# First layer of a four-layer image kernel: the projection streams the image over four column quadrants of TensorE, VectorE turns 32x32 blocks, and TensorE sums the squares

## The chip, the cores and the metric

One NeuronCore of a Trainium2 chip runs the whole program. The metric is the device time of one execution in microseconds (us); less is better. A NeuronCore has TensorE (PE in the rows; its weight loads are PEld), VectorE (DVE), ScalarE (ACT), GpSimd (POOL) and SyncE (SP), which run their own instruction streams and meet at semaphores. SBUF is the working memory of 128 partitions, PSUM the memory into which TensorE writes, in 8 banks of 512 fp32 values per partition.

## What is computed

Four layers in a row on an image `x` of 8 x 16 x 64 x 64 in fp32. Only layer 0, an attention along rows and along columns of the image, is touched by the change:

```python
x1 = (x - mu) / jnp.sqrt(var + EPS_LN) * ln_w[None, :, None, None] + ln_b[None, :, None, None]
out1 = _dwconv(x1, w01, b01) + _dwconv(x1, w11, b11) + _dwconv(x1, w21, b21)   # 1x7, 1x11, 1x21
out2 = _dwconv(x1, w02, b02) + _dwconv(x1, w12, b12) + _dwconv(x1, w22, b22)   # 7x1, 11x1, 21x1
out1 = _proj(out1, proj_w, proj_b)          # einsum 'bchw,oc->bohw', 16 x 16 channels
out2 = _proj(out2, proj_w, proj_b)
k1 = v1 = _split_h(out1); q1 = _split_h(out2)      # rows as tokens, 8 heads
k2 = v2 = _split_w(out2); q2 = _split_w(out1)      # columns as tokens
q1, k1, q2, k2 = (_l2norm(t) for t in (q1, k1, q2, k2))
attn1 = softmax(q1 k1^T); out3 = attn1 v1 + q1
attn2 = softmax(q2 k2^T); out4 = attn2 v2 + q2
return _proj(merge_h(out3)) + _proj(merge_w(out4)) + residual
```

Layers 1 and 3 are adaptive 9x9 blurs with an instance norm, layer 2 is a binarized 3x3 convolution. Their code is the same before and after.

## The kernel before

`build` calls the parts one after another, each in a block of its own that ends with a barrier of all engines: `l0_norm`, `l0_conv`, `l0_attention` (with `l0_out` at its end), `blur`, `binconv`, `blur`. Each engine's order within a block is written out by hand, with semaphores between the engines.

`l0_norm` loads x and the constants (ACT's DMAs at L301 and L304; a wait on all of them, `const_in`, stands ahead of ACT's squares at L308), normalises over the channels, builds the bias that the two convolutions and the projection add up to (`bias_lhs`, `bias_rhs`, two matmuls at L245, four small copies into `beta` at L343), and leaves two turned layouts of the image, `xrow` and `xcol`.

`l0_conv` has four steps.

1. Convolutions along rows and columns as products with Toeplitz matrices (L422), evacuated in turns by VectorE and ScalarE (L463).
2. Transposes back to image layout (L436), evacuated to `img[0]` and `img[1]` (L469, L472), which hold (channel, image) on the partitions and 64 x 64 pixels along each. In this stretch ScalarE and VectorE take turns again.
3. The projection (L450). It makes four tensors, of 8 jobs each, one job a PSUM bank: `xrow` and `o1c` from `img[0]`, `xcol` and `o2r` from `img[1]`. The result must have image pixels (the token's feature) on the partitions, so the image itself is the stationary operand: for each of a job's 8 planes a 128x64 piece of `img` is loaded as weights, twice (for each half `cp` of the output channels), and 64 columns of the 128x128 block matrix `projblk` are streamed through it. For `xrow` and `xcol` a plane is a contiguous image row, for `o1c` and `o2r` it is an image column, whose elements stand 64 apart (the `rearrange` of `planes`). VectorE adds the bias and puts each bank into the layout by heads (L500); PE may be four banks ahead (`proj_out, j - 3`).
4. The sums of squares for the L2 norms. ScalarE squares a finished tensor by heads (L483), VectorE sums 64 values of each (L494), interleaved with its evacuations of the next tensor, and after the last tensor eight more times; ScalarE has four buffers for that. Then one matmul adds the two partition halves and spreads the result (L456), VectorE takes the maximum with a small constant (L513), ScalarE the square root (L486), VectorE the reciprocal `rn` (L515). The block ends there and the attention begins.

The inner loop of step 3, and what sets its pace:

```python
pe.wait_ge(proj_out, j - 3)
...
mm = pe.matmul(ps[64 * cp:64 * cp + 64, j % 4, 64 * hh:64 * hh + 64],
               planes[:, ROWS * g + hh], projblk[:, 64 * cp:64 * cp + 64], start=True, stop=True)
```

The second argument of `pe.matmul` is stationary, the third moves; a row of the profile names the moving one first. An fp32 matmul stands in the trace as two MATMUL records and two LDWEIGHTS records.

Of the kernel before, what the change touches and what calls it, by code (L numbers as in the profile page):

```python
# [25 lines left out]
ALU = mybir.AluOpType  # L26
ACT = mybir.ActivationFunctionType

P = 128
B, C, H, W = 8, 16, 64, 64  # L30
HEADS = 8
# [40 lines left out]
def build(nc, d, band, out):  # L72

    keep = ExitStack()
    with keep:
# [18 lines left out]
        with ExitStack() as l0:  # L94
# [4 lines left out]
            pair = sb(l0, "pair", [P, P])  # L99
            rn = sb(l0, "rn", [P, HEADS * 16])  # L100
            beta = sb(l0, "beta_o", [P, 2, HEADS])
# [3 lines left out]
            with ExitStack() as ln:  # L105
                l0_norm(nc, sem, lambda n, s: sb(ln, n, s), d, ident, vec, pad_a, ps, x0,
                        xrow, xcol, toep, pair, beta, projblk, const_in, later, band, x_again)
            o1c = sb(l0, "o1c", [P, HEADS, B, W])
            o2r = sb(l0, "o2r", [P, HEADS, B, H])
            with ExitStack() as cv:  # L110
                l0_conv(nc, sem, lambda n, s: sb(cv, n, s), ident, pair, ps, xrow, xcol, toep, projblk,
                        beta, o1c, o2r, rn)
# [31 lines left out]
def l0_norm(nc, sem, sb, d, ident, vec, pad_a, ps, x0, xrow, xcol, toep, pair, beta,  # L144
# [11 lines left out]
    bias_rhs = sb("bias_rhs", [nb, C])  # L156
# [35 lines left out]
    with nc.Block() as block:  # L192
# [40 lines left out]
        def _(pe):  # L233
# [31 lines left out]
            pe.wait_ge(bias_read, 4)  # L265
# [34 lines left out]
        def _(act):  # L300
            act.dma_start(taps[:], d["taps"]).then_inc(taps_in, 16)  # L301
            for t, name in ((meansel, "meansel"), (ident, "ident"), (vec, "vec"), (bias_lhs, "bias_lhs"),
                            (bias_rhs, "bias_rhs"), (pair, "pair"), (mask, "mask"), (projblk, "projblk")):
                act.dma_start(t[:], d[name]).then_inc(const_in, 16)  # L304
# [24 lines left out]
        def _(dve):  # L329
# [10 lines left out]
            for t in range(2):  # L340
                for cp in range(CP):
                    src = ps[64 * cp:64 * cp + 64, 4, C * t:C * t + C].rearrange("p (n c) -> p c n", c=CP)
                    dve.tensor_copy(beta[64 * cp:64 * cp + 64, t, :], src[:, cp, :]).then_inc(bias_read, 1)  # L343
# [23 lines left out]
def l0_conv(nc, sem, sb, ident, pair, ps, xrow, xcol, toep, projblk, beta, o1c, o2r, rn):  # L367
# [9 lines left out]
    sqs = sb("sqs", [P, 4, BANK])  # L377
    ssum = sb("ssum", [P, 4, HEADS, B])
# [14 lines left out]
    proj_mm = sem("proj_mm")  # L393
    proj_out = sem("proj_out")
    squared = sem("q_squared")
    summed = sem("summed")
    nsq_mm = sem("nsq_mm")
# [6 lines left out]
    TENSORS = ((xrow, 2, 0, 0), (o1c, 1, 0, 1), (xcol, 0, 1, 0), (o2r, 3, 1, 1))  # L404
    NORM_BANK = 7
# [8 lines left out]
    with nc.Block() as block:  # L414
        @block.tensor
        def _(pe):
# [9 lines left out]
            for j in range(JOBS):  # L426
# [10 lines left out]
                mm.then_inc(turn_mm, 1)  # L437
            for i, (_, _, t, inner) in enumerate(TENSORS):
                planes = img[t][:] if inner == 0 else img[t][:].rearrange("p h w -> p w h")
                for g in range(CHUNKS):  # L440
# [3 lines left out]
                    else:  # L444
                        pe.wait_ge(proj_out, j - 3)
                    if i == 0 and g == 4:
                        wait_evacuated(pe, JOBS - 1, turn_v, turn_s)
                    for hh in range(ROWS):
                        for cp in range(CP):
# [5 lines left out]
            pe.wait_ge(summed, 4 * HEADS)  # L455
            pe.matmul(ps[:, NORM_BANK, 0:4 * HEADS * B], pair[:], ssum[:].rearrange("p t m b -> p (t m b)"),  # L456
                      start=True, stop=True).then_inc(nsq_mm, 1)
# [18 lines left out]
        def _(act):  # L476
            evacuate(act, act.copy, 1, conv_s, turn_s)
            for i in range(len(TENSORS)):
                act.wait_ge(proj_out, CHUNKS * (i + 1))
                for m in range(HEADS):  # L480
                    if HEADS * i + m >= 4:
                        act.wait_ge(summed, HEADS * i + m - 3)
                    act.activation(sqs[:, m % 4, :], TENSORS[i][0][:, m].rearrange("p b h -> p (b h)"),  # L483
                                   ACT.Square).then_inc(squared, 1)
            act.wait_ge(nsq_ready, CP)
# [3 lines left out]
        def _(dve):  # L489
            evacuate(dve, dve.tensor_copy, 0, conv_v, turn_v)  # L490
            def row_sums(i, m):

                dve.wait_ge(squared, HEADS * i + m + 1)
                dve.tensor_reduce(ssum[:, TENSORS[i][1], m, :], sqs[:, m % 4, :].rearrange("p (b h) -> p b h", b=B),  # L494
                                  mybir.AxisListType.X, ALU.add).then_inc(summed, 1)

            for i, (dst, _, t, _) in enumerate(TENSORS):
                for g in range(CHUNKS):
                    dve.wait_ge(proj_mm, CHUNKS * i + g + 1)
                    dve.tensor_tensor(dst[:, :, :, ROWS * g:ROWS * g + ROWS].rearrange("p m b h -> p h m b"),  # L500
                                      ps[:, g % 4, :].rearrange("p (h b m) -> p h m b", h=ROWS, b=B),
                                      spread(beta[:, t, :].unsqueeze(1).unsqueeze(3), [P, ROWS, HEADS, B]),
# [1005 lines left out]
```

## Time and profile before

| what | us |
|---|---|
| median of 3 runs (range) | 521.62 (521.18 to 524.71) |
| the profiled execution, its time | 524.1 |
| its span, first to last instruction | 522.3 |
| mean granted TensorE clock in it | 0.922 of 2.4 GHz |

The profile is of one execution. All rows count time from its span's start. In a view of groups, "x8" is the number of instructions, followed by busy time and the mean duration of one, then the idle time just before them and who ended it. In a timeline the first two numbers are start and length of a merged piece. In a table of stretches the columns are: stretch, length, busy us and count of PE, PEld, DVE, ACT, POOL, then the granted clock (1.00 is 2.4 GHz, 0.50 is 1.2 GHz), DMA share and GB/s.

### The profile page before, as it was taken

What the parts mean: (1) busy time and instruction counts of PE and PEld (TensorE: products, weight loads), DVE (VectorE), ACT (ScalarE), POOL (GpSimd) and SP (SyncE); (2) the same over time, 40 slices, a digit from 0 to 9 for tenths busy, and PEclk for the clock granted to TensorE, in tenths of its full rate; (3) what the DMA queues carried; (4) which work ended last, traced back from release to release, by engine and by line L of the source; (5) the groups of instructions that cost most, each with busy time, mean ns of one, the idle gap of its engine ahead of it and who ended that gap; (6) DMA issues with size and microseconds to landing.
All of it is one profiled execution on the core that took longest, in us unless ns stands there. A gap on an engine that the chain in (4) does not pass through costs nothing. (4 is left out here: it accounts for less than half of the span.)

```text
span 522.3 us, 18120 instructions
## 1 busy us (share of the span) xinstructions
PE 442.7 (85%) x7952; PEld 351.7 (67%) x7952; DVE 389.4 (75%) x597; ACT 264.3 (51%) x362; POOL 44.3 (8%) x64
## 2 busy tenths in 40 slices
PE   4588999994899919878999999849977899999971
PEld 2276999993799812255877778638745687777860
DVE  2795576987688895547899999847733889999963
ACT  0665432333333300038888888631105888888863
POOL 3320000000000000130000040000031000000000
PEclk9968999997799977969999999979996999999986
DMA  8830000000000000000000000000000000000004
GB/s 187 196 137 1 1 3 3 3 3 0 3 3 2 1 1 0 1 0 3 4 4 3 0 0 4 4 2 0 1 0 1 3 4 3 3 0 1 4 3 161
DMA packets 8093, 9.79 MB, mean 19 GB/s; under 512 B 5440, under 2 KB 6752, under 8 KB 7904
## 3 DMA queue, kind: packets, MB, share of 16 engines
q1 hardware_dynamic: 7008, 8.60, 5.8%
q8 instruction: 50, 0.82, 0.7%
q10 hardware_dynamic: 1024, 0.28, 0.3%
q14 instruction: 11, 0.09, 0.1%
HBM read 6.76 MB, written 2.11 MB: 17 GB/s over the span
## 5 line engine op out<-in xcount | busy, mean ns | idle before, releaser
L1068 DVE TENSOR_TENSOR g_wgt<-g_exponents,ps 128x1024 f32<-128x1024 f32 x128 | 151.0, 1205 | 5.0 <-PE ps L913 4.8
L1012 ACT ACTIVATE g_wgt<-g_wgt 128x1024 f32<-128x1024 f32 x128 | 132.4, 1061 | 18.7 <-DVE g_wgt L1068 17.9
L913 PE MATMUL ps<-ident,g_scl 128*128 128x128 f32 x512 | 80.3, 287 | 3.8 <-DVE g_scl L1059 3.6
L928 PEld LDWEIGHTS ps<-g_wgt,g_xt 128*32 128x32 f32 x4096 | 61.1, 111 | 21.7 <-issue 18.6
L928 PE MATMUL ps<-g_wgt,g_xt 128*32 128x64 f32 x4096 | 71.1, 222 | 2.7 <-issue 2.6
L913 PEld LDWEIGHTS ps<-ident,g_scl 128*128 128x128 f32 x512 | 57.3, 140 | 15.3 <-DVE g_scl L1059 4.9
L996 ACT ACTIVATE g_hid<-ps,vec 128x512 f32<-128x512 f32 x32 | 22.0, 688 | 66.0 <-PE ps L872 66.0
L450 PE MATMUL ps<-projblk,conv_img 128*64 128x64 f32 x1024 | 53.3, 266 | 0.7 <-DVE xcol L500 0.6
L450 PEld LDWEIGHTS ps<-projblk,conv_img 128*64 128x64 f32 x1024 | 52.7, 194 | 1.2 <-DVE xcol L500 1.1
L1309 PE MATMUL ps<-high,wb 128*128 128x512 f32 x72 | 30.2, 420 | 5.3 <-DVE rest L1338 5.3
L1309 PE MATMUL ps<-rest,wb 128*128 128x512 f32 x72 | 30.0, 417 | 0.0
L1019 ACT COPY g_num<-ps 128x512 f32<-128x512 f32 x32 | 18.5, 577 | 16.5 <-PE ps L928 16.4
L745 PE MATMUL ps<-xrow,outblk 128*64 128x512 f32 x32 | 16.0, 1070 | 11.9 <-DVE xcol L785 11.9
L624 ACT ACTIVATE e<-ps 128x512 f32<-128x512 f32 x16 | 9.6, 597 | 32.5 <-PE ps L586 32.5
L1005 ACT COPY g_xt<-ps 128x512 f32<-128x512 f32 x36 | 19.3, 585 | 11.3 <-PE ps L902 11.3
L1152 POOL COPY g_tile<-pad_b 128x512 f32 (+1 forms) x18 | 10.6, 617 | 151.2 <-PE ps L902 75.7
L872 PE MATMUL ps<-pad_b,g_w 128*128 128x512 f32 (+1 forms) x32 | 18.3, 655 | 5.5 <-ACT g_hid L996 2.0
L942 PE MATMUL ps<-ident,g_num 128*128 128x128 f32 x128 | 19.5, 275 | 3.8 <-ACT g_num L1019 3.8
L872 PE MATMUL ps<-pad_a,g_w 128*128 128x512 f32 (+1 forms) x32 | 18.3, 654 | 4.2 <-PEq L690 1.5
L902 PE MATMUL ps<-ident,g_tile 128*128 128x128 f32 x144 | 21.4, 291 | 0.1
L1152 POOL COPY g_tile<-pad_a 128x512 f32 (+1 forms) x18 | 10.6, 617 | 127.6 <-PE ps L902 74.3
L575 PE MATMUL ps<-ident,rnh 128*128 128x128 f32 x128 | 19.1, 297 | 2.5 <-POOL rnh L667 2.5
(156 smaller groups left out, 671.0 us busy)
## 6 DMA issues: line engine op xcount, KB each, us to landing
x<-in_x SPq DMA_DIRECT2D x8, 256.0 KB, 6.6
x<-in_x SPq DMA_DIRECT2D x1, 2048.0 KB, 8.6
out<-g_result SPq DMA_DIRECT2D x4, 512.0 KB, 3.9
windows<-band SPq DMA_DIRECT2D x4, 256.0 KB, 5.0
c_weight<-in_c_weight SPq DMA_DIRECT2D x1, 576.0 KB, 4.2
g_w<-in_g_w SPq DMA_DIRECT2D x2, 128.0 KB, 2.6
g_gband<-in_g_gband SPq DMA_DIRECT2D x2, 64.0 KB, 2.7
centre<-in_centre SPq DMA_DIRECT2D x1, 64.0 KB, 2.3
```

The lines of the kernel that those rows point to most:

```text
L450: mm = pe.matmul(ps[64 * cp:64 * cp + 64, j % 4, 64 * hh:64 * hh + 64], planes[:, ROWS * g + hh], projblk[:, 64 * cp:64 * cp + 64], start= ...
L872: pe.matmul(ps[:, MLP_BANK, :], w1[:, i, :], pad[:, rows, R:R + W], start=True, stop=True).then_inc(hid_mm, 1)
L902: tr = pe.transpose(ps[:, bank, P * j:P * j + P], tile[s][:, cb].rearrange("p r c -> p (r c)"), ident[:])
L913: tr = pe.transpose(ps[:, u % 4, P * k:P * k + P], spread(scl[s][:, k, u:u + 1], [P, P]), ident[:])
L928: mm = pe.matmul(ps[32 * j:32 * j + 32, O_BANK, 64 * cb:64 * cb + 64], xt[(s + t) % 2][:, cb, b, :], wgt[s][b][:, t, cb, :], start=(t == 0 ...
L942: tr = pe.transpose(ps[:, NT_BANK, P * k:P * k + P], num[i][:, P * k:P * k + P], ident[:])
L996: act.activation(hid[i][:].rearrange("p k r c -> p r k c"), ps[:, MLP_BANK, :].rearrange("p (r k c) -> p r k c", r=BLK, k=CB), ACT.Relu, b ...
L1005: act.copy(xt[s][:, 4 * k:4 * k + 4, :, 0:C], ps[:, (XT_BANK, MLP_BANK)[k], :].rearrange("p (k b m) -> p k b m", k=4, b=B)).then_inc(xt_ou ...
L1012: act.activation(w, w, ACT.Exp).then_inc(weight, 1)
L1068: dve.tensor_tensor(wgt[s][u][:], spread(gband[:].unsqueeze(2), shape), spread(s_in, shape), ALU.mult).then_inc(logit, 1)
L1152: ins = pool.tensor_copy(tile[s][:].rearrange("p (k o) r c -> p o k r c", o=2)[:, odd], cols.rearrange("p r (k c) -> p k r c", c=QC))
L1309: mm = pe.matmul(ps[:, g % 4, :], wb[:, t, :], part[:, ROWS * g + dh:ROWS * g + dh + ROWS, dw:dw + W], start=(k == 0), stop=(k == 2 * TAPS ...
```

## The change

Three things in `l0_conv`, and two that serve them in `l0_norm`.

- The projection swaps its operands. `projblk` is stationary, 32 of its columns at a time, and the image moves. A job's bank is filled by four matmuls of 512 columns, each into 32 partitions of it: two halves `cp` of the channels by two halves `side` of the other image axis. A job covers a strip of 16 lines and half of the images (`late`). For the two tensors that read `img` by columns the moving operand takes two neighbouring elements, then steps 64 (`lines`).
- The bank now has channels on its partitions. ScalarE adds the bias while it copies the bank to SBUF (`biased`, 4 buffers), and VectorE turns it by blocks of 32x32 into the layout by heads (`dve.transpose`).
- The squares go to ScalarE (heads 0, 1, 3, 4, 6) and GpSimd (heads 2, 5, 7), with eight buffers. TensorE sums them over the partitions: four matmuls with a one-hot column as weights for each half of a tensor, into four quadrants of one bank that collects all four tensors. After the last one VectorE copies that bank, TensorE turns it in four pieces, and VectorE takes the maximum from PSUM. The reductions on VectorE are gone.
- In `l0_norm` the bias is one small matmul and one copy, `pair` (128x128) is replaced by `onehot` (128x256), and `bias_rhs` grows from 49x16 to 49x128; both are loaded ahead of `const_in`.

```diff
@@ l0_norm
-            for t in range(2):
-                mm = pe.matmul(ps[:, 4, C * t:C * t + C], spread(bias_lhs[:, t:t + 1], [nb, P]),
-                               bias_rhs[:], start=True, stop=True)
-            mm.then_inc(bias_mm, 1)
+            pe.matmul(ps[:, 4, 0:2], bias_rhs[:], bias_lhs[:], start=True, stop=True).then_inc(bias_mm, 1)
...
+            dve.tensor_copy(beta[:], ps[:, 4, 0:2]).then_inc(bias_read, 1)
@@ l0_conv
+    TENSORS = ((xrow, 1, 0, 0), (o1c, 2, 0, 1), (xcol, 3, 1, 0), (o2r, 0, 1, 1))
+    SUM_BANK, NORM_BANK = 6, 7
+    STRIP = 16
+    ON_POOL = (2, 5, 7)
+    def lines(t, inner, strip, side):
+        across, along = slice(STRIP * strip, STRIP * strip + STRIP), slice(32 * side, 32 * side + 32)
+        if inner == 0:
+            return img[t][:, across, along]
+        return img[t][:, along, across].rearrange("p h (w o) -> p w h o", o=2)
...
+            def norm_sums(i, half):
+                heads = range(4 * half, 4 * half + 4)
+                pe.wait_ge(squared_p, len(ON_POOL) * i + sum(m <= heads[-1] for m in ON_POOL))
+                pe.wait_ge(squared_s, (HEADS - len(ON_POOL)) * i + sum(m not in ON_POOL for m in range(heads[-1] + 1)))
+                for m in heads:
+                    q = 32 * (m % 4)
+                    mm = pe.matmul(ps[q:q + 32, SUM_BANK, :], onehot[:, 2 * TENSORS[i][1] + half, :], sqs[:, m, :],
+                                   start=(i == 0 and half == 0), stop=(i == 3 and half == 1))
+                mm.then_inc(summed, 1)
...
-                        pe.wait_ge(proj_out, j - 3)
+                        pe.wait_ge(proj_biased, j - 3)
...
-                    for hh in range(ROWS):
-                        for cp in range(CP):
-                            mm = pe.matmul(ps[64 * cp:64 * cp + 64, j % 4, 64 * hh:64 * hh + 64],
-                                           planes[:, ROWS * g + hh], projblk[:, 64 * cp:64 * cp + 64],
+                    strip, late = divmod(g, 2)
+                    for cp in range(CP):
+                        for side in range(2):
+                            q = 64 * cp + 32 * side
+                            mm = pe.matmul(ps[q:q + 32, j % 4, :],
+                                           projblk[:, 64 * cp + 32 * late:64 * cp + 32 * late + 32],
+                                           lines(t, inner, strip, side),
                                            start=True, stop=True)
                     mm.then_inc(proj_mm, 1)
+                    if i > 0 and g % 4 == 3:
+                        norm_sums(i - 1, g // 4)
+            for half in range(2):
+                norm_sums(3, half)
+            pe.wait_ge(sums_out, 1)
+            for k in range(4):
+                tr = pe.transpose(ps[:, NORM_BANK, P * k:P * k + P], sums[:, P * k:P * k + P], ident[:])
+            tr.then_inc(nsq_mm, 1)
...
+                for m in ON_POOL:
+                    if i > 0:
+                        pool.wait_ge(summed, 2 * (i - 1) + m // 4 + 1)
+                    src = TENSORS[i][0][:, m].rearrange("p b h -> p (b h)")
+                    pool.tensor_tensor(sqs[:, m, :], src, src, ALU.mult).then_inc(squared_p, 1)
...
+            for i, (_, _, t, _) in enumerate(TENSORS):
+                for g in range(CHUNKS):
+                    j = CHUNKS * i + g
+                    act.wait_ge(proj_mm, j + 1)
+                    if j >= 4:
+                        act.wait_ge(proj_out, j - 3)
+                    act.activation(biased[:, j % 4, :], ps[:, j % 4, :], ACT.Identity, bias=beta[:, t:t + 1],
+                                   scale=1.0).then_inc(proj_biased, 1)
+                    if i > 0 and g not in ON_POOL:
+                        act_square(i - 1, g)
...
+                    dve.wait_ge(proj_biased, j + 1)
+                    dve.transpose(dst[:, :, HALF * late:HALF * late + HALF, STRIP * strip:STRIP * strip + STRIP]
+                                  .rearrange("p m b h -> p h b m"), block).then_inc(proj_out, 1)
```

`act_square(i, m)` waits for all eight jobs of tensor i (`proj_out`) and, from the second tensor on, for the sum that frees its buffer (`summed`).

How TensorE's order of `l0_conv` reads, from the Toeplitz products to the block's end. Before:

```order
L422 MATMUL ps<-xrow,toep 128x256 x16
L422 MATMUL ps<-xcol,toep 128x256 x16
L436 MATMUL ps<-ident,xrow 128x128 x32
L436 MATMUL ps<-ident,xcol 128x128 x32
L450 MATMUL ps<-projblk,conv_img 64x64 x512
L456 MATMUL ps<-ssum,pair 128x256
L414 UNCONDITIONAL_BRANCH
```

And now, from the last transposes on (the pattern of 16 and 4 goes on for the third and fourth tensor):

```order
L443 MATMUL ps<-ident,xcol 128x128 x32
L469 MATMUL ps<-conv_img,projblk 32x512 x48
L452 MATMUL ps<-sqs,onehot 32x512 x4
L469 MATMUL ps<-conv_img,projblk 32x512 x16
L452 MATMUL ps<-sqs,onehot 32x512 x4
L469 MATMUL ps<-conv_img,projblk 32x512 x16
...
L469 MATMUL ps<-conv_img,projblk 32x512 x16
L452 MATMUL ps<-sqs,onehot 32x512 x12
L480 MATMUL ps<-ident,norm_sums 128x128 x4
```

The 512 short matmuls are 128 long ones; the first twelve jobs stand in a row (48 matmuls), and from there on every fourth job is followed by a group of four sums, which TensorE cannot pass before the squares of the tensor before are there.

ScalarE's order in the same block, from the evacuations of the transposes on (`sqs` are the squares, `biased` the banks with their bias). Before:

```order
L469 COPY conv_img<-ps 128x512 x4
L472 COPY conv_img<-ps 128x4x2x64 x4
L483 ACTIVATE sqs<-xrow 128x512 x8
L483 ACTIVATE sqs<-o1c 128x512 x8
L483 ACTIVATE sqs<-xcol 128x512 x8
L483 ACTIVATE sqs<-o2r 128x512 x8
L486 ACTIVATE root<-nsq 128x128
```

And now:

```order
L506 COPY conv_img<-ps 128x4x2x64 x4
L526 ACTIVATE biased<-ps,beta_o 128x512 x9
L516 ACTIVATE sqs<-xrow 128x512
L526 ACTIVATE biased<-ps,beta_o 128x512
L516 ACTIVATE sqs<-xrow 128x512
L526 ACTIVATE biased<-ps,beta_o 128x512 x2
L516 ACTIVATE sqs<-xrow 128x512
L526 ACTIVATE biased<-ps,beta_o 128x512
L516 ACTIVATE sqs<-xrow 128x512
L526 ACTIVATE biased<-ps,beta_o 128x512 x2
L516 ACTIVATE sqs<-xrow 128x512
L526 ACTIVATE biased<-ps,beta_o 128x512 x2
```

A bank's evacuation now stands on ScalarE, and between the evacuations of one tensor stand five squares of the tensor before; the first of them comes right after the ninth evacuation.

## Rows read from the trace of the kernel before

**Rows 1.** Busy time by stretch, from the first projection job to the attention's start.

```profile
67.60:75.20 7.60, 7.60 (x259) 7.59 (x260) 6.75 (x8) 0.59 (x1) 0.00 (x0) 1.00 0.02 4
75.20:94.10 18.90, 18.90 (x269) 18.90 (x267) 11.92 (x17) 4.95 (x8) 0.00 (x0) 1.00 0.01 2
94.10:106.00 11.90, 11.21 (x301) 10.79 (x298) 11.90 (x17) 4.61 (x8) 0.00 (x0) 1.00 0.01 3
...
122.00:133.00 11.00, 2.22 (x7) 1.50 (x8) 7.54 (x13) 5.82 (x12) 0.47 (x6) 0.56 0.00 0
```

**Rows 2.** Groups of instructions by line, 67.6 to 133 us.

```profile
L450 PE MATMUL ps<-projblk,conv_img 128*64 128x64 f32 x1024 | 53.3, 266 | 0.7 <-DVE xcol L500 0.6
...
L494 DVE TENSOR_REDUCE ssum<-sqs 128x8 f32<-128x512 f32 x32 | 20.5, 659 | 0.2 <-ACT sqs L483 0.2
```

**Rows 3.** Timeline of the end of the stage, 121 to 132 us.

```profile
121.64 1.01 DVE L500 TENSOR_TENSOR o2r<-ps,beta_o 128x512 f32<-128x512 f32 x1 [0.80 <-PE ps L450]
...
122.69 4.27 ACT L483 ACTIVATE sqs<-o2r 128x512 f32<-128x512 f32 x8 [8.17 <-DVE o2r L500]
...
128.24 1.22 PE L456 MATMUL ps<-ssum,pair 128*128 128x256 f32 x2 [6.64 <-DVE ssum L494]
129.50 0.61 DVE L513 TENSOR_SCALAR nsq<-ps 64x128 f32<-64x128 f32 x2 [1.31 <-PE ps L456]
130.14 0.31 ACT L486 ACTIVATE root<-nsq 128x128 f32<-128x128 f32 x1 [3.19 <-DVE nsq L513]
130.48 0.95 DVE L515 RECIPROCAL rn<-root 128x128 f32<-128x128 f32 x1 [0.38 <-ACT root L486]
```

**Rows 4.** Timeline of PE at L253, matmuls of 512 columns into four quadrants.

```profile
16.38 2.13 PE L253 MATMUL ps<-sq,meansel 128*32 128x512 f32 x16
```

**Rows 5.** The same view, in the stretch from 17.5 to 18.2 us.

```profile
17.26 1.24 PE L253 MATMUL ps<-sq,meansel 128*32 128x512 f32 x8
```

**Rows 6.** Timeline of layer 0's output projection, in 64-column halves.

```profile
196.97 2.00 PE L745 MATMUL ps<-xrow,outblk 128*64 128x512 f32 x4 [11.94 <-DVE xcol L785]
...
198.75 1.93 PE L749 MATMUL ps<-xcol,outblk 128*64 128x512 f32 x4
...
203.05 2.00 PE L745 MATMUL ps<-xrow,outblk 128*64 128x512 f32 x4
...
204.84 1.08 PE L749 MATMUL ps<-xcol,outblk 128*64 128x512 f32 x4
```

**Rows 7.** Timeline of operations like those added, and of PE after an idle time.

```profile
13.13 4.27 ACT L308 ACTIVATE sq<-xc 128x512 f32<-128x512 f32 x8 [2.02 <-DMA projblk<-in_projblk]
...
21.81 3.60 POOL L223 TENSOR_TENSOR toep<-windows,mask 128x2048 f32<-128x2048 f32 x1 [16.66 <-DMA windows<-band]
...
25.66 1.09 PE L270 MATMUL ps<-ident,wide 128*128 128x128 f32 x4 [5.76 <-DVE wide L296]
...
44.75 3.65 PE L422 MATMUL ps<-xrow,toep 128*128 128x256 f32 x8 [2.60 <-PEq L192]
...
187.52 7.47 DVE L771 STREAM_TRANSPOSE xrow<-attn_c 128x512 f32<-128x512 f32 x8
```

**Rows 8.** Granted clock of stretches, all engines.

```profile
44.80:48.20 3.40, 3.40 (x8) 2.72 (x9) 0.69 (x1) 0.00 (x0) 0.00 (x0) 0.50 0.02 5
0.00:13.10 13.10, 6.12 (x10) 2.71 (x11) 3.23 (x6) 1.28 (x1) 4.62 (x5) 1.00 0.85 187
```

**Rows 9.** The same, PE alone: stretch, length, busy (count), clock, DMA.

```profile
200.00:201.00 1.00, 1.00 (x4) 0.50 0.00 0
202.00:203.00 1.00, 1.00 (x6) 1.00 0.00 0
227.00:230.00 3.00, 2.03 (x10) 0.50 0.00 0
```

**Rows 10.** One line's instructions: ns least, median, most; first and last start.

```profile
L785 DVE STREAM_TRANSPOSE xcol<-attn_r x8: 997/1007/1252, 194.9 to 210.4; 128x512 f32<-128x512 f32 x8
```

**Rows 11.** Groups of ACT by line.

```profile
L996 ACT ACTIVATE g_hid<-ps,vec 128x512 f32<-128x512 f32 x32 | 22.0, 688 | 66.0 <-PE ps L872 66.0
```

More of the change, by code:

```diff
@@ L106, in build @@
                 l0_norm(nc, sem, lambda n, s: sb(ln, n, s), d, ident, vec, pad_a, ps, x0,
-                        xrow, xcol, toep, pair, beta, projblk, const_in, later, band, x_again)
+                        xrow, xcol, toep, onehot, beta, projblk, const_in, later, band, x_again)
             o1c = sb(l0, "o1c", [P, HEADS, B, W])
@@ L110, in build @@
             with ExitStack() as cv:
-                l0_conv(nc, sem, lambda n, s: sb(cv, n, s), ident, pair, ps, xrow, xcol, toep, projblk,
+                l0_conv(nc, sem, lambda n, s: sb(cv, n, s), ident, onehot, ps, xrow, xcol, toep, projblk,
                         beta, o1c, o2r, rn)
@@ L263, in _ @@
                 tr.then_inc(var_turned, 1)
-            pe.wait_ge(bias_read, 4)
+            pe.wait_ge(bias_read, 1)
             for t in range(PXT):
@@ L364, in _, with l0_conv @@
                     dve.tensor_copy(turned_out(lay, g), turned_in(g)).then_inc(evac_v, 1)
-def l0_conv(nc, sem, sb, ident, pair, ps, xrow, xcol, toep, projblk, beta, o1c, o2r, rn):
+def l0_conv(nc, sem, sb, ident, onehot, ps, xrow, xcol, toep, projblk, beta, o1c, o2r, rn):
     img = [sb(f"conv_img{t}", [P, H, W]) for t in range(2)]
-    sqs = sb("sqs", [P, 4, BANK])
-    ssum = sb("ssum", [P, 4, HEADS, B])
+    biased = sb("biased", [P, 4, BANK])
+    sqs = sb("sqs", [P, HEADS, BANK])
+    sums = sb("norm_sums", [P, BANK])
     nsq = sb("nsq", [P, HEADS, 4, HALF])
@@ L506, in _ @@
-            for m in range(HEADS):
-                row_sums(3, m)
+            for i, (dst, _, _, inner) in enumerate(TENSORS):
+                for g in range(CHUNKS):
+                    j = CHUNKS * i + g
+                    strip, late = divmod(g, 2)
+                    block = biased[:, j % 4, :].rearrange("p (a h q) -> p a h q", a=STRIP // 2, h=2) if inner == 0 else \
+                        biased[:, j % 4, :].rearrange("p (a q h) -> p a h q", a=STRIP // 2, h=2)
+                    dve.wait_ge(proj_biased, j + 1)
+                    dve.transpose(dst[:, :, HALF * late:HALF * late + HALF, STRIP * strip:STRIP * strip + STRIP]
+                                  .rearrange("p m b h -> p h b m"), block).then_inc(proj_out, 1)
@@ L509, in _ @@
+            dve.wait_ge(summed, 2 * len(TENSORS))
+            dve.tensor_copy(sums[:], ps[:, SUM_BANK, :]).then_inc(sums_out, 1)
             dve.wait_ge(nsq_mm, 1)
-            for odd in range(2):
-                part = slice(64 * odd, 64 * odd + 64)
-                sums = ps[part, NORM_BANK, 0:4 * HEADS * B].rearrange("p (t m k o) -> p o m t k", t=4, m=HEADS, o=2)
-                dve.tensor_scalar(nsq[part], sums[:, odd], L2_EPS_SQ, None, ALU.max).then_inc(nsq_ready, 1)
+            found = ps[:, NORM_BANK, :].rearrange("p (k q r) -> p q k r", k=4, q=4)[:, :, :, 0:8]\
+                .rearrange("p q k (t u) -> p u q t k", u=2)
@@ L514, in _ @@
+            for u in range(2):
+                dve.tensor_scalar(nsq[:, 4 * u:4 * u + 4], found[:, u], L2_EPS_SQ, None, ALU.max).then_inc(nsq_ready, 1)
             dve.wait_ge(norm_ready, 1)
```

65 lines of the change are left out of this document (26 added, 39 removed).

## The prediction

> **What bounds the kernel now.** I read the table of stretches first, then the groups by line of the stage that is changed, then its timeline. The stage runs from the first projection matmul at 67.6 us to the end of the reciprocal `rn` at 130.48 + 0.95 = 131.43 us [rows 3]: 63.8 us, an eighth of the span. In its first and second stretch PE and its weight loads are busy all the time while VectorE and ScalarE are not [rows 1]. The second tensor (image columns as weights) takes 18.9 us for what the first did in 7.6 us; both are 128 matmuls of 64 columns, so 148 against 59 ns each, and what differs is the strided weight load. In the third stretch VectorE is busy for all of 11.9 us: per job one evacuation and one reduction. The fourth tensor is again strided. In all, PE is busy 53.3 us with L450 and VectorE 20.5 us with the reductions [rows 2]. Then PE stands still, and the end is a chain: last evacuation (121.64), eight squares with their reductions (122.69), one matmul (128.24), maximum, root, reciprocal [rows 3], 9.8 us in all. The attention needs `rn`, so every us of this stage is a us of the kernel. Nothing else in the program changes its work.
>
> **Prices.** A job in quadrants: at L253 two groups of four matmuls, each 512 columns into 32 partitions, start at 16.38 and 17.26 [rows 4, 5], so 0.88 us for four; I use 0.87. Four quadrants do run side by side when the moving operand is contiguous. About 0.2 us pass from a group's last column to the next engine (the two groups last 2.13, not 1.76 us), the handoff of 0.04 us between engines (122.65 to 122.69 [rows 3]) included.
>
> ScalarE's evacuation with a bias from PSUM: 0.69 us [rows 11], its square 8 in 4.27, so 0.53 each and some 0.1 more for the last [rows 7]. I take 0.60 and 0.53 in a row. A tensor then costs ScalarE 8 x 0.60 + 5 x 0.53 = 7.5 us.
>
> VectorE's block transpose of 128x512: 7.47 us for 8, 0.93 each [rows 7], up to 1.25 in another place [rows 10]. Those read strided and write contiguously; the new ones write single values far apart, which no row shows. Bounds 0.93 and 1.5 (the slowest, and as much again as it lies above its median); I take 0.95 in a row, 1.0 for the last, by the nearer row. A tensor costs VectorE 7.6 us in place of up to 11.9.
>
> GpSimd's square of 512: a product of 2048 took 3.60 us [rows 7], so 0.90; bounds 0.9 and 1.9 (twice, if it and VectorE get in each other's way), taken 0.95. It has 5 us before anybody needs them, except at the end.
>
> The strided jobs are the open price. L745 moves an operand with single values 128 bytes apart into two halves: 203.05 to 204.84, 1.79 us for the pair at the full clock, and 196.97 to 198.75, 1.78 us at half the clock [rows 6, 9]. So the reads set that pace, not the array: twice the 0.87 us. The new operand takes two neighbours at a time. If a stream is held to one access per value pair, the pairs bring it back to 0.87. If instead all streams together are held to a number of accesses, four streams of pairs need as many as two of singles, 1.78 us. If neighbours help nothing, four streams need twice L745's, 3.56 us. Bounds 0.87 and 3.56, taken 0.87.
>
> The Trainium skill bears on this: SBUF — State Buffer, section "Door 1: The DMA port swizzle", says that reads come in lines of 16 bytes and that each stream needs at least two hits in a line for full bandwidth. L745's half pace agrees with it. By that rule the pairs run at full pace, the 0.87 us that I take.
>
> **The sum, as a chain.** It starts at 67.6 us as before.
>
> 1. First tensor: first bank ready 67.6 + 0.87 + 0.2, ScalarE 0.69, then eight transposes of 0.95: 77.0 us. PE has by then filled three or four banks of the second tensor.
> 2. ScalarE's next instructions are in the order square, evacuation, square, evacuation, evacuation, square: 3.6 us, to 80.6. Only then can PE pass the first sums. It has waited some 2.5 us.
> 3. From a tensor's first sums to its second: sums 0.87, three jobs 2.61, handoff 0.22, evacuation 0.60, square 0.62, handoff 0.05: 4.97 us. To 85.6.
> 4. From the second sums to the next tensor's first: sums 0.87, one job 0.87, handoff 0.22, four evacuations 2.40, three squares 1.68, handoff 0.05: 6.09 us. A period is thus 11.06 us (PE is busy for ten groups of 0.87, 8.7, and waits 2.3). Two periods: 107.7.
> 5. The last bank: evacuation 0.69 and transpose 1.0 after it, to 109.4. ScalarE's last five squares end at 112.2, GpSimd's three at 112.3.
> 6. Two groups of sums, the first begun at 111.1. PE has idled 3 us, so at half clock, 1.74 each: 114.8. Copy of the bank by VectorE 0.74, an estimate from ScalarE's 0.69 [rows 11]: 115.5. Four transposes at half clock 1.09 [rows 7]: 116.6. Maximum 0.66, root 0.36, reciprocal 1.0 [rows 3]: 118.6.
>
> 131.4 - 118.6 = 12.8 us gained. Tail for tail nothing is won: it was 9.8 us and is 9.2.
>
> Against it: the larger constants. ScalarE's first squares wait for the last of them (`projblk`) at 13.13 [rows 7]; 64 KB and 22 KB more at the 187 GB/s of the stretch before it [rows 8] are 0.5 us, and the norm's chain hangs on it: 0.4 us. The bias's three fewer copies lie beside that chain, nothing. And PE's clock: after 2.60 us idle [rows 7] it stood at 1.2 GHz from 44.8 to 48.2 us, 3.4 us in all [rows 8]. The wait of step 2 is as long. In 3.4 us at half clock two groups pass instead of four: 1.7 us. I count one such drop; the shorter waits of steps 3 and 4 (0.5 and 1.7 us) may add one each or none.
>
> 12.8 - 0.4 - 1.7 = 10.7 us. The profiled execution took 524.1 us with a span of 522.3, so it would take 513.4. It stood 2.5 us above the median of 521.6; against the median the forecast is 510.9 us. The own range of this case is 507 (no drop, cheap starts) to 515 (three drops, transposes at 1.25).
>
> **Rivals.**
>
> - *Pairs at half pace* (1.78 us per strided job). For: rows 6 can't tell a limit per stream from one over all, and the contiguous quadrants fit both. The second and fourth tensor then take 5.5 and 6.1 us more and the last bank 0.9; without waits the clock's 1.7 us come back. 10.7 - 12.5 + 1.7 = 0: 521.7 us, no change.
> - *VectorE becomes the bound*: a transpose over 11.06 / 8 = 1.38 us. At 1.5 us the first tensor ends 4.4 us later and each of the other three takes 1 us more: 518.6 us.
> - *The clock stays down* (slower). It falls in step 2 and the waits between sums keep it there. For: at the start of the first blur PE was two thirds busy, 2.03 of 3 us, and stayed at 1.2 GHz [rows 9]. Against: at half clock a group takes 1.74 us, PE has hardly any wait left, and steady work brought the clock back from 0.50 at 200 us to 1.00 at 202 us [rows 9]. The periods would be 18.9 us (ten groups of 17.4 and two short waits) instead of 11.06: 15.7 us more for two, 3.5 for the first tensor's sums, about 1 at the end. 10.7 + 1.7 - 20.2 = -7.8: 529.4 us. It decides against the change from about two thirds of the stage at half clock. The Trainium skill knows such a pattern (TensorE: Matmul & The Clock Gate, "A second HAM failure mode: psum-queue depth-cycling": short idles between groups of matmuls let the clock swing); by it this rival gains, while the second stretch of rows 1 shows no such waits to judge it by.
> - *Neighbours help nothing*, 3.56 us per strided job (slower too): 16 jobs by 2.7 us, of which waits hide little: some 41 us, less the 1.7: 550 us. The change loses from 1.9 us per strided job on.
>
> **How the numbers follow.** Forecast 0.66, half pace 0.14, VectorE or GpSimd slower 0.06, clock down 0.08, neighbours nothing 0.06. Faster by over 1% (below 516.4 us; about what a measurement tells from no change): 0.66 and a third of the 0.06, 0.68. Slower by over 1%: 0.14. Between: 0.18. The range is 507 to 522.5 us: it reaches over the half pace's 521.7 and leaves out the two slower cases and a little below. GpSimd at 1.9 us would add 3 us at the end, which lies inside.
>
> **What would show it.** Right: records of the strided jobs' groups 0.87 us apart as the contiguous ones; `rn` written at about 119 us on the old time scale; PE waiting on ScalarE's squares before each group of sums, longest before the first; transposes around 1.0 us; the clock at 0.50 only after that first wait and at the end. Wrong: strided jobs 1.78 us apart (the gain gone), transposes above 1.38 us with ScalarE waiting for VectorE, or a clock of 0.50 through the second to fourth tensor.

## The result, and the profile after

| | before | after |
|---|---|---|
| median of 20 runs each (range), us | 523.37 (519.85 to 525.95) | 518.27 (512.84 to 521.99) |
| ratio after to before, 95% interval | | 0.9888 (0.9862 to 0.9913) |
| profiled execution, time and span | 524.1, 522.3 | 518.3, 516.5 |
| mean granted clock in it | 0.922 | 0.931 |

The ratio leaves out the six of the change's 20 runs that took over 1.5% more than its fastest; over all runs the medians differ by 5.1 us, 1.0%.

The kernel became faster by 1.0 to 1.1%, some 5 to 6 us, where 10.7 us were forecast. The measured time lies inside the stated range (507 to 522.5) but outside the forecast's own (507 to 515). It does so also on the forecast's own base: 0.9888 of 521.6 us is 515.8 us. The gain is about half of what was forecast: the prediction was wrong in size, right in sign.

The busy time by stretch of the changed kernel's profile, cut at the ends of the four tensors (columns as in [rows 1]):

```profile
67.70:77.70 10.00, 10.00 (x87) 3.55 (x90) 8.49 (x10) 7.78 (x10) 0.00 (x0) 1.00 0.01 2
77.70:89.70 12.00, 9.98 (x70) 3.36 (x66) 8.71 (x9) 8.00 (x12) 3.18 (x3) 1.00 0.00 0
89.70:101.50 11.80, 9.65 (x85) 3.11 (x81) 8.78 (x8) 7.48 (x13) 3.03 (x3) 1.00 0.01 1
101.50:115.00 13.50, 11.12 (x75) 3.78 (x67) 8.85 (x9) 8.72 (x13) 3.71 (x3) 1.00 0.00 0
115.00:123.50 8.50, 4.15 (x20) 1.02 (x20) 2.00 (x4) 3.02 (x6) 3.03 (x3) 0.80 0.01 2
```

No engine is full after the first tensor, and the clock stands at 2.4 GHz until the tail. PE's weight loads, all of the time busy in [rows 1], are down to a third. What sets the pace is read from PE's timeline, where each piece of the projection is four jobs (x32 records) and each L452 a group of sums:

```profile
81.49 1.07 PE L452 MATMUL ps<-sqs,onehot 128*32 128x512 f32 x8 [1.73 <-ACT sqs L516]
...
82.35 5.43 PE L469 MATMUL ps<-conv_img,projblk 128*32 128x512 f32 x32
...
88.07 1.07 PE L452 MATMUL ps<-sqs,onehot 128*32 128x512 f32 x8 [0.29 <-ACT sqs L516]
...
88.93 3.64 PE L469 MATMUL ps<-conv_img,projblk 128*32 128x512 f32 x32
...
94.17 1.07 PE L452 MATMUL ps<-sqs,onehot 128*32 128x512 f32 x8 [1.60 <-ACT sqs L516]
...
95.03 3.64 PE L469 MATMUL ps<-conv_img,projblk 128*32 128x512 f32 x32
...
99.22 1.07 PE L452 MATMUL ps<-sqs,onehot 128*32 128x512 f32 x8 [0.55 <-ACT sqs L516]
...
100.08 5.29 PE L469 MATMUL ps<-conv_img,projblk 128*32 128x512 f32 x32
```

Four contiguous jobs last 3.64 us, four strided ones 5.29 to 5.43. Less the 0.17 us of the last one's drain that is 0.87 and 1.3 us a job. The sums wait for ScalarE's squares, 1.5 to 1.7 us ahead of a tensor's first group (forecast: 2.5 once, then 1.7) and 0.3 to 0.55 ahead of its second (forecast 0.5). The tail, which answers to [rows 3]:

```profile
115.03 2.71 ACT L516 ACTIVATE sqs<-o2r 128x512 f32<-128x512 f32 x5 [1.14 <-DVE o2r L546]
115.07 3.03 POOL L491 TENSOR_TENSOR sqs<-o2r 128x512 f32<-128x512 f32 x3 [9.75 <-DVE o2r L546]
...
116.84 3.49 PE L452 MATMUL ps<-sqs,onehot 128*32 128x512 f32 x16 [2.32 <-ACT sqs L516]
...
120.38 0.69 DVE L550 COPY norm_sums<-ps 128x512 f32<-128x512 f32 x1 [5.39 <-PE ps L452]
...
121.12 0.66 PE L480 MATMUL ps<-ident,norm_sums 128*128 128x128 f32 x4 [0.79 <-DVE norm_sums L550]
121.82 0.36 DVE L555 TENSOR_SCALAR nsq<-ps 128x64 f32<-128x64 f32 x2 [0.75 <-PE ps L480]
122.21 0.31 ACT L534 ACTIVATE root<-nsq 128x128 f32<-128x128 f32 x1 [4.47 <-DVE nsq L555]
122.55 0.95 DVE L557 RECIPROCAL rn<-root 128x128 f32<-128x128 f32 x1 [0.38 <-ACT root L534]
```

The reciprocal ends at 123.50, not at 118.6. Two groups of sums of 0.87 us each take 3.49 us because the clock has just fallen (mean 0.80 in the last stretch, 0.50 from 118.0 to 120.3 us). That is as forecast here, but three repetitions below kept the full clock at this place.

Lastly, what the other engines paid. The views of one line give least, median and most in ns; here the evacuations on ScalarE and the transposes into two of the tensors:

```profile
L526 ACT ACTIVATE biased<-ps,beta_o x32: 659/688/1482, 68.9 to 113.2; 128x512 f32<-128x512 f32 x32
...
L546 DVE STREAM_TRANSPOSE xrow<-biased x8: 1083/1115/1392, 69.6 to 76.6; 128x512 f32<-128x512 f32 x8
L546 DVE STREAM_TRANSPOSE o1c<-biased x8: 1054/1070/1715, 77.6 to 88.6; 128x512 f32<-128x512 f32 x8
```

```profile
L491 POOL TENSOR_TENSOR sqs<-xcol x3: 1074/1332/1555, 101.6 to 104.2; 128x512 f32<-128x512 f32 x3
```

The medians of ScalarE and VectorE are near what was priced: 0.69 us for an evacuation, and transposes that overlap and so start 0.96 us apart in the first six of `xrow` (0.95 was taken). But some of either take up to twice as long, and GpSimd's squares up to half as long again as the 1.04 us that they take beside a contiguous stream. The slow ones stand where PE moves the strided operand: those of `xrow` come after 74.6 us, when PE is already at the second tensor.

### The profile page after: what moved, and what is told of

Read it like the earlier page. It is cut to its first block and busy times, and to the rows that moved or that the text cites. A ratio compares the mean times of both kernels' runs of the same rounds, so it can differ in the third digit from the quotient of the medians.

```text
span 516.5 us, 16761 instructions
## 1 busy us (share of the span) xinstructions
PE 431.7 (84%) x7248; PEld 311.4 (60%) x7248; DVE 374.6 (73%) x563; ACT 279.2 (54%) x382; POOL 57.2 (11%) x76
## 5 line engine op out<-in xcount | busy, mean ns | idle before, releaser
L955 PE MATMUL ps<-ident,g_scl 128*128 128x128 f32 x512 | 78.9, 283 | 4.5 <-DVE g_scl L1101 3.6
L970 PE MATMUL ps<-g_wgt,g_xt 128*32 128x64 f32 x4096 | 72.6, 223 | 7.5 <-issue 7.4
L970 PEld LDWEIGHTS ps<-g_wgt,g_xt 128*32 128x32 f32 x4096 | 62.0, 111 | 27.2 <-issue 24.1
L469 PE MATMUL ps<-conv_img,projblk 128*32 128x512 f32 x256 | 35.4, 673 | 0.0
L526 ACT ACTIVATE biased<-ps,beta_o 128x512 f32<-128x512 f32 x32 | 23.5, 746 | 13.6 <-PE ps L469 13.5
L1194 POOL COPY g_tile<-pad_b 128x512 f32 (+1 forms) x18 | 10.6, 617 | 156.1 <-POOLq L1340 80.7
L469 PEld LDWEIGHTS ps<-conv_img,projblk 128*32 128x32 f32 x256 | 12.7, 112 | 20.3 <-issue 15.5
```

The lines of the kernel that those rows point to most:

```text
L469: mm = pe.matmul(ps[q:q + 32, j % 4, :], projblk[:, 64 * cp + 32 * late:64 * cp + 32 * late + 32], lines(t, inner, strip, side), start=Tru ...
L526: act.activation(biased[:, j % 4, :], ps[:, j % 4, :], ACT.Identity, bias=beta[:, t:t + 1], scale=1.0).then_inc(proj_biased, 1)
L955: tr = pe.transpose(ps[:, u % 4, P * k:P * k + P], spread(scl[s][:, k, u:u + 1], [P, P]), ident[:])
L970: mm = pe.matmul(ps[32 * j:32 * j + 32, O_BANK, 64 * cb:64 * cb + 64], xt[(s + t) % 2][:, cb, b, :], wgt[s][b][:, t, cb, :], start=(t == 0 ...
L1194: ins = pool.tensor_copy(tile[s][:].rearrange("p (k o) r c -> p o k r c", o=2)[:, odd], cols.rearrange("p r (k c) -> p k r c", c=QC))
```

## The experiments

Each ran beside the kernel before on the same chip. "Stage" is the time from the first projection matmul to the end of `rn`: 63.8 us before, 55.8 in the change's first profile.

### How many neighbours a strided stream needs

In all of these the operand of the strided tensors is cut otherwise, with VectorE's block following; the diff shows it for four neighbours.

```diff
-        return img[t][:, along, across].rearrange("p h (w o) -> p w h o", o=2)
+        return img[t][:, along, across].rearrange("p h (w o) -> p w h o", o=4)
...
-                        biased[:, j % 4, :].rearrange("p (a q h) -> p a h q", a=STRIP // 2, h=2)
+                        biased[:, j % 4, :].rearrange("p (a q h) -> p a h q", a=4, h=4)
```

**Singles (o=1).** 

> The strided jobs move single values 64 apart instead of pairs of neighbours; the bank's order and VectorE's blocks follow. Theory A (all moving streams together are held to a number of accesses, an access serving neighbours up to one line): four streams of singles need twice the accesses of pairs, so a strided job goes from 1.29 us (measured in the change) to 2.6 us or, at L745's rate of 1.79 us for two streams, 3.6 us; rn comes some 16 to 28 us later than in the change. Theory B (each stream has its own limit and the pairs meet it; the 1.29 us come from collisions with what ScalarE and VectorE read and write at the time): 1.7 to 2.1 us per job, rn 6 to 10 us later. Contiguous jobs stay at 0.86 us in both.

PE's timeline, four strided jobs in the second tensor and four in the fourth:

```profile
86.08 9.56 PE L469 MATMUL ps<-conv_img,projblk 128*32 128x512 f32 x32
...
108.09 10.33 PE L469 MATMUL ps<-conv_img,projblk 128*32 128x512 f32 x32
```

2.35 and 2.54 us a job (less the last one's drain): between the two theories' numbers, nearer to A's 2.6, and far from the 3.6 us that a common limit at L745's rate would give. `rn` at 140.1, 16.6 later; the one run took 533.1 us, 10 us over the kernel before. Without neighbours the change would have lost.

**Fours (o=4).** 

> Four neighbours at a time. Theory A: half the accesses of pairs, strided jobs fall from 1.29 to 0.87 us, rn about 4.8 us earlier than in the change (118.7 on its time scale). Theory B: the collisions with the other engines stay in part, 1.0 to 1.29 us per job, rn 0 to 3 us earlier. Third possibility: VectorE's transposes, which now read their source with a stride of 16 bytes, become slower than 1.02 us; above 1.38 us each they take the gain back.

Strided jobs that ran at the full clock took 0.89 to 0.94 us. But the run was no faster than the change: stage 57.3 us, 519.7 us in all. PE's timeline and the clock (PE, weight loads, DVE, ACT, POOL, clock) show why:

```profile
79.48 1.06 PE L452 MATMUL ps<-sqs,onehot 128*32 128x512 f32 x8 [2.70 <-ACT sqs L516]
80.34 5.45 PE L469 MATMUL ps<-conv_img,projblk 128*32 128x512 f32 x32
```

```profile
80.70:84.10 3.40, 3.40 (x20) 1.19 (x16) 1.18 (x1) 1.48 (x3) 0.00 (x0) 0.50 0.00 0
104.60:108.00 3.40, 3.40 (x20) 1.09 (x19) 0.98 (x1) 0.00 (x0) 0.00 (x0) 0.50 0.00 0
```

With the faster jobs PE reached the sums earlier and waited 2.70 us for the squares, and from 80.7 us on it had 1.2 GHz for 3.4 us; the same again in the fourth tensor after 2.14 us. This is the clock drop that the forecast had put into the change itself, where PE waited only 1.73 us. The fours don't leave the other engines undisturbed either: VectorE's transposes of `o1c` took up to 2017 ns. What the reads gave, the clock and these took; how much each did, this one run doesn't tell.

**Sixteen (o=16, the whole strip in a row).** 

> All sixteen values of a strip in a row (64-byte runs), VectorE reads its source with a stride of 64 bytes. Theory A: as with four neighbours, 0.87 us per strided job, rn at 118.7, total about 4 to 5 us under the change, ratio to before 0.978 to 0.982. Theory B: also near 0.87 us, but falling on from four to sixteen. If VectorE's read stride costs, transposes above 1.02 us, visible first in the second and fourth tensor; under 1.38 us they stay hidden but for the last.

```profile
81.36 3.64 PE L469 MATMUL ps<-conv_img,projblk 128*32 128x512 f32 x32
...
97.56 3.64 PE L469 MATMUL ps<-conv_img,projblk 128*32 128x512 f32 x32
```

The strided jobs are now as fast as the contiguous ones, 3.64 us for four. The slow evacuations and transposes are gone with them, and the source stride of 64 bytes costs VectorE nothing:

```profile
L526 ACT ACTIVATE biased<-ps,beta_o x32: 672/687/693, 68.6 to 107.6; 128x512 f32<-128x512 f32 x32
...
L546 DVE STREAM_TRANSPOSE o1c<-biased x8: 1043/1104/1151, 76.8 to 86.2; 128x512 f32<-128x512 f32 x8
```

Stage 49.6 us, 6.2 less than the change. PE waited 2.52 us ahead of the first sums and this time kept the clock. This run is also the test of the forecast's chain, since its strided jobs have the 0.87 us that the chain took. From the first projection matmul to the first sums it took 13.0 us (forecast 13.0), and then from sums to sums 5.05, 6.11, 5.04, 6.11 and 5.05 (forecast 4.97 and 6.09 in turns).

The whole time shows less: median 514.1 us of 4, ratio to before 0.987 (0.980 to 0.995), where 0.978 to 0.982 was expected. The change's own 0.989 lies in that interval, so the gain over the change is shown for the stage and not for the kernel.

**Two streams in place of four, in pairs.** The loop over `side` runs once, so half of each bank isn't computed.

> Leaves out the matmuls of side 1: two of the four quadrants of each bank are not computed, so two streams run in place of four, in pairs of neighbours. Theory A: half the accesses, strided jobs 0.87 us. Theory B and any limit per stream: 1.1 to 1.29 us as with four streams. Contiguous jobs 0.87 us in both.

```profile
82.12 4.43 PE L469 MATMUL ps<-conv_img,projblk 128*32 128x512 f32 x16
...
98.87 4.34 PE L469 MATMUL ps<-conv_img,projblk 128*32 128x512 f32 x16
```

1.04 to 1.07 us a job. Half the accesses did not bring it to 0.87, so the limit is not one over all streams alone; nor is it one per stream alone, since four streams take 1.3. Even two streams of pairs don't run free. Both theories as written fall. The other engines ran undisturbed: no evacuation took over 749 ns, no transpose over 1146. The two streams that are left move the same values, the left-out ones the other half, so the number of streams and the amount of different data were changed together. What exactly the limit is stays open.

### The wait for the squares

**Sixteen neighbours, sums two jobs later.**

```diff
-                    if i > 0 and g % 4 == 3:
-                        norm_sums(i - 1, g // 4)
-            for half in range(2):
+                    if i > 0 and g == 5:
+                        norm_sums(i - 1, 0)
+                    if i > 1 and g == 1:
+                        norm_sums(i - 2, 1)
+            norm_sums(2, 1)
+            for half in range(2):
```

> As the run with sixteen neighbours, and each group of sums stands two jobs later in TensorE's order (after the sixth job of the next tensor, and after the second of the one behind it), so that TensorE finds the squares ready. Theory (the period is set by the wait of TensorE for ScalarE's squares, 1.7 us and 0.5 us per period): the waits go, the period falls from 11.1 us to what VectorE's transposes set, 8 x 1.02 to 1.08 = 8.2 to 8.7 us, three periods give 7 us; rn at about 110 us. Rival (what the sums cost is TensorE's own time or VectorE's and ScalarE's work, not the wait): the period stays above 10 us and rn comes at 115 or later. Total: 7 us under the run with sixteen neighbours if the first holds, ratio to before 0.972 to 0.978.

```profile
85.37 1.07 PE L452 MATMUL ps<-sqs,onehot 128*32 128x512 f32 x8
...
86.23 3.64 PE L469 MATMUL ps<-conv_img,projblk 128*32 128x512 f32 x32
...
89.66 1.07 PE L452 MATMUL ps<-sqs,onehot 128*32 128x512 f32 x8
...
93.95 1.07 PE L452 MATMUL ps<-sqs,onehot 128*32 128x512 f32 x8
```

No wait stands at these groups, and from one tensor's sums to the next one's (85.37 to 93.95) it is 8.6 us, where the change took 11.2 to 14.2 (from 88.07 to 99.22, and from 99.22 to 113.45). VectorE is busy 8.04 of 8.40 us in the third tensor:

```profile
86.10:94.50 8.40, 8.40 (x84) 3.00 (x80) 8.04 (x9) 7.48 (x13) 3.04 (x3) 1.00 0.01 2
```

`rn` at 110.57, stage 42.5 us, as the first theory has it. Median 504.8 us of 6 runs, ratio 0.966 (0.963 to 0.970), better than the 0.972 to 0.978 expected and 17.5 us under the kernel before: this version beats both.

**Pairs, sums two jobs later** (the same edit on the change itself).

> The change with its pairs, only the sums two jobs later. If the strided jobs' pace is the second bound beside the wait: the strided tensors' periods are 8 x 1.15 to 1.3 plus 1.7 = 11 to 12 us (14.2 in the change), the contiguous ones about 8.7; rn 4 to 7 us earlier than in the change (123.5). If the wait was all: as with sixteen neighbours, rn near 110.

`rn` at 113.74, stage 47.6 us, 8.2 less than the change and more than was expected; one run of 506.3 us. In the stage the wait alone was worth more (8.2 us) than the reads alone (6.2). With the reads mended too another 5.1 us come off.

**One part of the change alone: squares and sums in their new places, the old projection.**

> The kernel before with one part of the change alone: squares on ScalarE and GpSimd, sums on TensorE, the old projection and its evacuation kept. Theory (the reductions on VectorE cost only where VectorE was the bound, the third tensor, and the sums put 0.87 us a group on TensorE, the bound of the second and fourth): third tensor 9.3 to 10 us instead of 11.9, second and fourth 1.7 us longer each; rn 0 to 4 us later than before (131.4). Rival (the reductions were a good part of the stage's cost): rn 4 us or more earlier than before.

`rn` at 135.95, stage 68.2 us: 4.4 us slower than before, a little over what the theory gave. One run of 526.4 us. PE carries 17.08 us for the first tensor and half of the second, and then the sums on top:

```profile
67.73 17.08 PE L464 MATMUL ps<-projblk,conv_img 128*64 128x64 f32 x384
84.74 1.06 PE L448 MATMUL ps<-sqs,onehot 128*32 128x512 f32 x8
```

So the whole gain needs the projection's new form. Whether it needs the new sums too isn't shown: the new projection with the reductions left on VectorE wasn't run. An estimate from the rows: eight transposes 0.96 us apart and eight reductions of 0.66 [rows 2] would keep VectorE busy for 13 us a tensor, against periods of 11.2 to 14.2 in the change.

### What lies behind `rn`

Repetitions of both kernels, for the places of the clock and the rest of the program. The expectations of the five runs, in order (the first names a wait of 2.2 to 2.7 us ahead of the first sums; it was 1.73 us in all four profiles of the change):

> The changed kernel once more, for its clock. If the 2.2 to 2.7 us in which TensorE waits ahead of the first sums are at the edge of what the clock bears, another execution can show 1.2 GHz within the stage, as the run with four neighbours did at 80.7 us, and rn later than 123.5 by 1 to 4 us; if the stage's clock is the same in each, rn is within 0.5 us of 123.5, and the spread of the total comes from behind it.

> The kernel before once more, for what lies behind rn. In its first profile 390.9 us passed from rn to the end, in the two of the change 393.0 and 390.2. Theory (the rest is the same work and only meets the clock differently in each execution): the time from rn to the end lies anywhere between 389 and 394 us, with the stretches at 1.2 GHz in other places. Rival (the earlier rn gives something back behind it): close to 390.9 here, and above 392 in the change.

> The changed kernel for a third time. Same theories: from rn to the end 389 to 394 us, or above 392. Its stage from the first projection matmul to rn 55 to 56 us, if the clock holds in it; 57 to 59 if TensorE's wait ahead of the first sums costs the clock this time.

> The kernel before a third time: stage 63.8 us from the first projection matmul to rn, and from rn to the end 389 to 394 us (same work, clock differs) or close to 390.9 (rival).

> The changed kernel a fourth time: stage 55 to 56 us with the clock held, 57 to 59 without; from rn to the end 389 to 394 us (same work, clock differs) or above 392 (rival).

| us | before, 3 profiles | change, 4 profiles |
|---|---|---|
| whole execution | 524.1, 524.7, 522.3 | 518.3, 515.1, 519.3, 514.9 |
| stage | 63.8, 63.8, 63.8 | 55.8, 55.3, 56.0, 55.5 |
| `rn` to the first blur's first matmul | 89.3, 89.4, 89.6 | 88.3, 88.2, 88.4, 88.2 |
| from there to layer 2's first | 126.7, 126.9, 126.8 | 128.2, 127.4, 127.5, 127.4 |
| from there to the end | 174.8, 175.0, 174.9 | 176.5, 174.6, 178.1, 175.5 |
| `rn` to the end | 390.9, 391.2, 391.3 | 393.0, 390.2, 394.0, 391.0 |

The stage repeats within 0.7 us, 8.2 us less on average, but not by the same parts. The three repetitions keep the full clock to `rn`, so their tail (from the third tensor's second sums to `rn`) is 9.0 to 9.1 us in place of 10.05. But two of their three strided steps are longer (7.2 and 8.0 to 8.5 us against 6.6 and 7.6), though PE's four jobs in the first of them took 5.05 us against 5.43. The second of them in the third profile of the change:

```profile
100.44 5.10 PE L469 MATMUL ps<-conv_img,projblk 128*32 128x512 f32 x32
...
108.05 1.06 PE L452 MATMUL ps<-sqs,onehot 128*32 128x512 f32 x8 [2.51 <-ACT sqs L516]
...
117.96 1.07 PE L452 MATMUL ps<-sqs,onehot 128*32 128x512 f32 x8 [2.32 <-ACT sqs L516]
```

From sums to sums it is 8.5 us here (99.58 to 108.05), while PE's four jobs took 5.10. A transpose of 2657 ns and an evacuation of 1801 stand in this stretch, and ScalarE's squares, on which the sums wait, come later. What the strided operand costs thus lies in the other engines as much as in PE.

Behind `rn` both theories are half right: the change's times scatter over 4 us while those of before don't, and on average they are 0.9 us longer. Unchanged code gives back 2.1 us after the attention had gained 1.2. One difference there is the wait of PE for its own issue in L928 (L970 after); columns are waited-for us in total, times, longest. Before and after:

```profile
PE ps L928 <- issue: 2.6, 2, 1.3
```

```profile
PE ps L970 <- issue: 7.4, 6, 1.9
```

All three profiles of before have 2.6 to 3.0 us of them, all four of the change 7.3 to 8.2, at the end of each blur. At the first blur's end VectorE waits for PE, and in the first profile the clock is at 1.2 GHz from 332.1 us on:

```profile
DVE g_rzb L1117 <- PE ps L984: 7.8, 2, 5.0
```

```profile
332.10:345.80 13.70, 7.63 (x22) 0.50 0.00 1
```

Before, the first of these rows had 3.5 us, and the stretch at 1.2 GHz at this place lasted 6.8 us in all three profiles; in the four of the change it lasted 10.2 or 13.7.

That these waits make the time behind `rn` isn't shown, and other runs speak against them as the only cause. They were 5.6 us with sixteen neighbours, where `rn` to the end took 391.9 us, and 5.2 us with the sums alone, where it took 388.6, less than before the change. The latter has the old projection with all its matmuls, so having fewer matmuls ahead is not what brings the waits either.

Two more runs asked whether it is the place of that code in PE's stream. Both put idle instructions into `l0_norm`, where PE waits 5 us anyway, and nothing else:

```diff
+            for _ in range(24):
+                pe.nop(nofuse=True)
             pe.wait_ge(bias_read, 1)
```

> The changed kernel with 24 idle instructions in TensorE's stream, in l0_norm where TensorE waits 5 us for ScalarE and VectorE anyway. Theory (place in the stream): the waits for issue in the blurs' ends, 7.3 to 8.2 us in 6 to 8 places in four runs of the change, move to other instructions and add up to something else, by 1 us or more; stage still 55.5 us. Rival (not the place): 7.3 to 8.2 us at the same instructions.

> The same with 80 idle instructions. Theory: again another sum, and if the places follow the padding, the first long wait comes at an instruction some 56 further back in the code than with 24. Rival: 7.3 to 8.2 us at the same instructions as without padding.

5.7 us in 6 places with 24, 6.9 us in 7 with 80: the sums moved somewhat, but the waits stood at the same matmuls as without padding (with 24, one of the first blur's four, 1.4 to 1.9 us in the change, was missing). So a shift of up to 80 instructions doesn't move them. What brings them stays open; the differences between the programs weren't taken back one by one. The time from `rn` to the end was 392.8 us with 24 and 391.0 with 80, so here too the smaller waits don't go with the shorter time. The whole times were 517.6 and 518.4 us. The stage was 55.3 us with 24 but 57.3 with 80, where 55.5 was expected: with 80 the clock fell in the tail and stayed at 1.2 GHz to `rn`.

## Why the prediction was wrong, point by point

- *What bounds the kernel before*: right. The strided weight loads were the cost, and the run with the sums alone shows that nothing is gained while they stay.
- *Four quadrants side by side, 0.87 us a job*: right for the contiguous jobs, to 0.01 us.
- *Strided jobs, taken at 0.87 us between bounds of 0.87 and 3.56*: this is the step that failed. They took 1.3 us with four streams. Steps 3 and 4 of the chain were priced at 4.97 and 6.09 us. In the contiguous third tensor they took 5.05 (94.17 to 99.22) and 6.10 (88.07 to 94.17); where the streams are strided 6.58 and 7.62 (81.49 to 88.07, 99.22 to 106.84), and 6.61 once more (to 113.45). The excess of the three together is 4.8 us, nearly all of the 4.9 that `rn` came late; in the three repetitions it is 5.3 to 6.1. The run with sixteen neighbours shows it as the cause: with 0.87 us a job the same steps took 5.05 and 6.11.
- The forecast had two clean cases, full pace and half pace, and the truth lay between. It also held the operand's cost to PE, while it slowed ScalarE, VectorE and GpSimd too. The Trainium skill's rule (SBUF — State Buffer, "Door 1: The DMA port swizzle") of two hits in a 16-byte line would have made pairs free; here pairs cost 1.3 us against 0.87, and the measurement decides.
- *Transposes 0.95*: right, 0.96 where PE reads contiguously. *The first sums*, forecast 13.0 us after the first projection matmul, came 13.8 after it (81.49). This is the same step again: with sixteen neighbours it was 13.0.
- *The tail*, forecast 10.9 us from the third tensor's second sums on, took 10.05 with the half clock where it was put, and 9.0 to 9.1 in the three repetitions, which kept the full clock. What was too dear even in the first profile are the four transposes (0.66 us at the full clock, priced 1.09) and the maximum (0.36, priced 0.66).
- *The clock*, one drop of 1.7 us in step 2: it did not come in the four profiles of the change (the wait was 1.73 us, since the strided jobs were slow), and came twice with four neighbours. The wait of 2.52 us with sixteen, longer than the 2.5 of the forecast, cost no clock. So a wait can bring the drop, but its length alone doesn't tell whether it does.
- *Constants*, 0.4 us: not seen. The first projection matmul began at 66.5 to 67.8 us in four profiles of the change, and at 65.5 to 67.9 in three of the kernel before.
- *Behind `rn`*: the forecast carried the saving to the end unchanged. It lost 0.9 us on average. So 12.8 us forecast in the stage were 8.2, and of these about 7 arrive in the profiles; the medians of 20 runs show 5 to 6. The last one or two us between profiles and medians are not explained.
- *Luck*: two charges against the gain, 1.7 us for the clock and 0.4 for the constants, did not fall due, and the tail was cheaper than priced. They hid a part of what the strided jobs cost. That the time lies inside the stated range is owed to the rival at half pace, for which the range was widened, and not to the forecast's own chain.
- *Rivals*: pairs at half pace would have given no gain, neighbours without use a loss. The gain of 5 to 6 us lies about halfway between the forecast's 10.7 and the first rival's 0, as the 1.3 us of a job lie between 0.87 and 1.78. VectorE never became the bound in the change; it is nearly that (8.04 of 8.40 us busy) only with sixteen neighbours and the later sums.

## What to carry to other kernels

Swapping operands so that a strided image moves instead of being loaded as weights pays, if the moving stream takes runs of neighbours and the next engine sorts them out: sixteen in a row cost VectorE's transposes nothing here. When several engines alternate over the same banks, an in-order wait of TensorE two jobs too early can cost more than slow reads do, here 8.2 us against 6.2; move it until it finds its input ready. Price a strided operand not only for the engine that moves it, but for those that read and write the same memory beside it. And price a step that makes an engine faster together with the wait it then runs into: with fours the clock fell after two such waits.

## What the runs showed of the hardware

- Four streams of 512 fp32 columns, full clock: 2.2 to 2.5 us with single values, 1.2 to 1.3 with pairs, 0.89 to 0.94 with fours, 0.87 with sixteen or 32 in a row; two streams of pairs 1.04 to 1.07.
- While TensorE moved pairs, ScalarE's evacuation took up to 1482 ns (at most 693 with sixteen), VectorE's transpose up to 1715 (1153), and GpSimd's square up to 1555 (1043); in a repetition the first two took up to 1801 and 2657. These engines work on other tiles than TensorE reads. In which part of the memory they meet, no run shows.
- TensorE kept the full clock over waits of 1.73 us each time, and of 2.52 us twice in the run with sixteen. It fell to 1.2 GHz after 2.70 and 2.14 us with fours. After the wait of 2.32 us in the tail it fell in one profile of the change and not in two others.
